# Perceiver layer with top-2 experts on one core: the first seven parts of the output copy put out one at a time

## The chip, the cores and the metric

One core of one Trainium2 chip runs the whole kernel. The metric is the device time of one execution in microseconds (us). Times of the kernel before are the median of three runs; the profile and the trace come from one further execution, taken by the hardware profiler.

## What is computed

The input x is 64 sequences of 64 tokens of 256 numbers, so 4096 tokens. Three blocks with a residual each follow one another, all in float32:

```python
x = x + xattn(layernorm(x), ctx_768, Wq, Wk, Wv, Wo, bo)  # 16 heads of 64, context 256 x 192 per sequence
x = x + attn(layernorm(x), wq, wk, wv, wo)                # causal, 16 heads of 64
x = x + ffn(layernorm(x), router, gating, up, down)       # 8 experts, the 2 likeliest per token, SiLU(gate) * up, then down
```

In the ffn block each token's result is the sum of its two experts' results, each scaled by its weight.

## The kernel before

The work goes through three stages. In the first (cross attention, to about 1090 us) and the second (self attention with the router, to about 1925 us) the tokens go through in tiles of 128. The second stage leaves two things in HBM for the third. `acc` is an array of all tokens with their residual values, to which the experts' results are added. `xs` holds the normalized token rows sorted by expert, each expert's rows in the order of the tokens, each row with its token number and its weights as tags.

The third stage is the function `moe`, in which the change lies. It runs over 67 tiles of 128 rows of `xs`, expert by expert; how many tiles an expert has is found on the chip and read from small tables in SBUF with `value_load`. The engines share it as follows.

- SP (the sync engine's queue) loads the tiles. Before it loads a tile it waits (line 1773, 1776 or 1780) until the Vector engine has copied an earlier one out of the two-tile buffer `e_xs_in`, so it keeps step with the computation until the very last tile; two loads past the last tile close the series (lines 1779 to 1781).
- PE (TensorE), ACT (ScalarE) and DVE (VectorE) compute each tile's gate, up and down products. ACT writes the weighted result to one half of `e_ys` (line 1909), after a wait until POOL has taken the token numbers of the tile before (`s_out_now`, line 1908).
- POOL (GpSimd) adds each tile's 128 result rows to `acc` with one indirect DMA that accumulates (line 1808, called "an add" from here on). It begins with a wait for the add before it to land (line 1799), so that the adds form a chain. Each add raises the semaphore `s_added` (`e_ys_added`) by 16 when it has landed.
- SP, when all its loads are out, copies `acc` to the output `out_x` in eight parts of 512 tokens, 512 KB each, from HBM to HBM (lines 1784 to 1793, "parts" from here on, numbered 0 to 7). Before each part it reads from the table `part_done` how many adds must have landed before those tokens are final, and waits for that count on `s_added`. This can be before the last add, since the last expert's rows are in the order of the tokens. Part 7 waits for all adds. A last wait holds until all eight parts have landed (`s_out`, line 1793).

`part_done` is worked out on the Vector engine at the end of the second stage (lines 1657 to 1662). SP's order is that of the program: what stands behind a wait isn't issued until the wait is over. DMAs that SP has issued are in flight together.

Of the kernel before, what the change touches and what calls it, by code (L numbers as in the profile page):

```python
# [28 lines left out]
DMA = 16  # L29
PARTS_OUT = 8  # L30
# [1638 lines left out]
def moe(nc, sem, sbuf, psum, xs_dram, s_scat, ident, raw, s_raw, load_piece, split, pads, tables, shape, acc,  # L1669
# [26 lines left out]
    with ExitStack() as ph:  # L1696
# [4 lines left out]
        with ExitStack() as ex:  # L1701
# [23 lines left out]
            s_weight, s_out_now, s_out = sem("e_weight_kept"), sem("e_token_out_set"), sem("out_stored")  # L1725
            out_gate, s_out_gate = sbuf(ex, "e_out_gate", [P, 1]), sem("e_out_gate_done")

            def tile_count(eng):
                return eng.value_load(first_tile[0:1, EXPERTS:EXPERTS + 1], min_val=MIN_TILES * EXPERTS, max_val=MAX_TILES)
# [23 lines left out]
            @block.sync  # L1753
            def _(sp):
                def load_tile(i, row, landed):
                    sp.dma_start(xs_in[:, bass.ds(i % 2 * ROW, ROW)],
                                 xs_tiles[bass.ds(row, 1)].rearrange("t p r -> p (t r)")).then_inc(landed, DMA)

                sp.wait_ge(s_scat, (4 * GROUPS + 1) * DMA)
                load_tile(0, 0, s_xs)  # L1760
                load_tile(1, 1, s_xs_second)
                sp.wait_ge(s_wlo, PIECES)
                for c in range(PIECES):
                    load_piece(sp, 1, c)
                start = 0
                for e in range(EXPERTS):
                    bound = dict(min_val=MIN_TILES * (e + 1), max_val=MAX_TILES - MIN_TILES * (EXPERTS - 1 - e))
                    end = sp.value_load(first_tile[0:1, e + 1:e + 2], **bound)
                    shift = sp.value_load(region[0:1, e:e + 1], min_val=0, max_val=(TILES + 1) * e) if e else 0
                    if e == 1:  # L1770
                        sp.wait_ge(s_scat, DMA * (4 * GROUPS + EXPERTS))
                    for i in range(0 if e else 2, MIN_TILES):
                        sp.wait_ge(s_moved, start + i)
                        load_tile(start + i, start + i + shift, s_xs)
                    with sp.Fori(start + MIN_TILES, end) as i:
                        sp.wait_ge(s_moved, i)
                        load_tile(i, i + shift, s_xs)
                    start = end
                for i in range(2):
                    sp.wait_ge(s_moved, start + i)  # L1780
                    load_tile(start + i, i, s_xs)
                for c in range(PIECES):
                    sp.wait_ge(s_raw[c], DMA * EXPERTS)
                part = NTOK // PARTS_OUT
                for c in range(PARTS_OUT):
                    if c + 1 < PARTS_OUT:
                        sp.wait_ge(s_added, sp.value_load(part_done[0:1, c:c + 1], min_val=DMA * MIN_TILES * (EXPERTS - 1),
                                                          max_val=DMA * MAX_TILES))
                    else:
                        sp.wait_ge(s_added, DMA * tile_count(sp))  # L1790
                    sp.dma_start(out[c * part:(c + 1) * part, :].rearrange("(b r) d -> b (r d)", b=32),
                                 acc[c * part:(c + 1) * part, :].rearrange("(b r) d -> b (r d)", b=32)).then_inc(s_out, DMA)
                sp.wait_ge(s_out, PARTS_OUT * DMA)
# [221 lines left out]
```

## Time and profile before

| what | us |
|---|---|
| median of three runs | 2300.44 |
| lowest and highest run | 2297.36, 2302.71 |
| the profiled execution's own time | 2298.02 |
| its span in the trace | 2296.3 |
| PE busy | 2176.0 (95%) |
| DVE busy | 1555.2 (68%) |
| ACT busy | 1301.2 (57%) |
| POOL busy | 914.2 (40%) |

The span is what lies between the first and the last event of the trace; the execution's own time is 1.7 us longer. The busy shares are means over all three stages. The change touches only the last 30 us, after the last load of a tile, and in those last 30 us PE's work comes to its end.

### The profile page before, as it was taken

The numbers are of one execution on the slowest core, as the hardware profiler recorded it, in microseconds if no ns is written. First come the engines' busy times: TensorE is split into PE (matmuls) and PEld (weight loads), VectorE is DVE, ScalarE is ACT, GpSimd is POOL, SyncE is SP. The second block draws the span as 40 slices with busy tenths as digits, with TensorE's granted clock in tenths as the row PEclk, the third lists the DMA queues.
The fourth block names the chain that finished last, engine by engine and source line by source line (L and its number), as shares of the span: only waits on it lengthen the run. The fifth ranks groups of instructions, "written<-read, shape, count | busy, mean of one in ns | idle before, by whom it ended". The sixth has DMA issues, their size and how long they took to land. (4 is left out here: it accounts for less than half of the span.)

```text
span 2296.3 us, 56727 instructions
## 1 busy us (share of the span) xinstructions
PE 2176.0 (95%) x19008; PEld 1980.3 (86%) x19008; DVE 1555.2 (68%) x3525; ACT 1301.2 (57%) x3925; POOL 914.2 (40%) x1409
## 2 busy tenths in 40 slices
PE   6999999999999999999996999999999994999996
PEld 5899999999999999999995899999999983888885
DVE  6666676767676666667654888888888874444442
ACT  5555555555555555555553777777677762545442
POOL 3333333333333333333332225555555554444443
PEclk9999999999999999999997999999999996999998
DMA  4000000000000000000005200000000003444434
GB/s 120 22 20 28 9 27 18 27 11 25 27 18 27 9 27 18 27 9 27 14 6 172 104 11 16 22 21 19 23 19 21 22 25 105 100 82 97 81 63 108
DMA packets 63901, 93.55 MB, mean 41 GB/s; under 512 B 6824, under 2 KB 47144, under 8 KB 63528
## 3 DMA queue, kind: packets, MB, share of 16 engines
q1 hardware_dynamic: 44280, 64.49, 8.8%
q0 software_dynamic: 13104, 18.56, 4.6%
q10 hardware_dynamic: 6432, 9.44, 1.4%
q8 instruction: 44, 0.72, 0.1%
q14 instruction: 41, 0.34, 0.0%
HBM read 65.39 MB, written 36.83 MB: 45 GB/s over the span
## 5 line engine op out<-in xcount | busy, mean ns | idle before, releaser
L424 POOL TENSOR_TENSOR p_sb<-p_sb,rinv 128x512 f32<-128x512 f32 x256 | 279.0, 1090 | 780.0 <-DVE rinv L770 780.0
L679 ACT ACTIVATE p_sb<-s_ps,nmax 128x256 f32<-128x256 f32 x512 | 238.1, 470 | 198.7 <-DVE nmax L745 194.9
L745 DVE TENSOR_REDUCE nmax<-s_ps 128x2 f32<-128x512 f32 x256 | 176.1, 688 | 186.1 <-PE s_ps L67 181.7
L1090 POOL TENSOR_TENSOR sp_sb<-sp_sb,srinv 128x512 f32<-128x512 f32 x128 | 133.1, 1040 | 228.8 <-DVE srinv L1444 226.7
L1340 ACT ACTIVATE sp_sb<-sm_sb,snmax 128x128 f32<-128x128 f32 x512 | 199.6, 391 | 5.6 <-DVE snmax L1459 2.6
L767 DVE COPY pt_sb<-t_ps 128x512 f32<-128x512 f32 x256 | 176.8, 690 | 22.2 <-PE t_ps L567 8.4
L48 ACT ACTIVATE q_sb<-m_ps 64x256 fp32r<-64x256 f32 x256 | 96.8, 378 | 164.4 <-PE m_ps L67 160.6
L47 ACT CAST qk_hi<-qk_ps 128x512 fp32r<-128x512 f32 x218 | 129.6, 595 | 95.6 <-PE qk_ps L67 87.7
L567 PE MATMUL t_ps<-ident,p_sb 128*128 128x128 f32 x1024 | 153.6, 273 | 2.1 <-POOL p_sb L424 1.1
L67 PE MATMUL sqk_ps<-e_w_hi 128*128 128x256 f32 x512 | 147.8, 289 | 7.2 <-DVE e_w_lo L59 7.2
L567 PEld LDWEIGHTS t_ps<-ident,p_sb 128*128 128x128 f32 x1024 | 125.1, 141 | 31.6 <-issue 4.4
L650 ACT COPY v_sb<-v_ps 128x512 f32<-128x512 f32 x256 | 149.4, 584 | 1.5 <-PE v_ps L67 1.5
L67 PE MATMUL s_ps<-cx_hi,qk_hi 128*128 128x256 f32 x512 | 148.2, 289 | 0.0
L67 PE MATMUL sqk_ps<-e_w_lo,e_w_hi 128*128 128x256 f32 x512 | 145.5, 284 | 0.0
L67 PE MATMUL sqk_ps<-e_w_hi,e_w_lo 128*128 128x256 f32 x512 | 145.4, 284 | 0.0
L67 PE MATMUL qk_ps<-q_sb,wkt_hi 128*128 128x256 f32 x436 | 131.4, 323 | 14.3 <-DVE qk_hi L59 5.9
L67 PE MATMUL s_ps<-cr_lo,qk_hi 128*128 128x256 f32 x512 | 144.9, 283 | 0.0
L67 PE MATMUL s_ps<-cx_lo,qk_hi 128*128 128x256 f32 x512 | 144.8, 283 | 0.0
L67 PE MATMUL s_ps<-cx_hi,qk_lo 128*128 128x256 f32 x512 | 144.6, 283 | 0.0
L67 PE MATMUL s_ps<-cr_hi,qk_hi 128*128 128x256 f32 x512 | 144.6, 282 | 0.0
L583 PEld LDWEIGHTS o_ps<-pt_sb,v_sb 128*64 128x64 f32 x4096 | 126.1, 139 | 11.5 <-issue 10.5
L583 PE MATMUL o_ps<-pt_sb,v_sb 128*64 128x64 f32 x4096 | 135.0, 225 | 0.8 <-DVE pt_sb L767 0.8
(340 smaller groups left out, 7465.7 us busy)
## 6 DMA issues: line engine op xcount, KB each, us to landing
e_xs_in<-xs SPq DMA_DIRECT2D x69, 132.5 KB, 2.1
ctx_raw<-in_ctx_t SPq DMA_DIRECT2D x32, 256.0 KB, 2.8
ctx_raw<-in_ctx_t SPq DMA_DIRECT2D x64, 128.0 KB, 2.9
xs<-blank_rows SPq DMA_DIRECT2D x8, 662.5 KB
x_ring<-in_x SPq DMA_DIRECT2D x16, 256.0 KB, 2.8
x_mid<-x_ring SPq DMA_DIRECT2D x16, 256.0 KB, 2.2
acc<-x_sb SPq DMA_DIRECT2D x16, 256.0 KB, 2.1
out_x<-acc SPq DMA_DIRECT2D x8, 512.0 KB, 5.3
```

The source lines that it names most:

```text
L47: return nc.scalar.copy(hi, src)
L48: return nc.scalar.mul(hi, src, scale)
L67: mm = pe.matmul(out, lhs, rhs, start=(i == 0), stop=(i == len(pairs) - 1))
L424: nc.gpsimd.tensor_tensor(prob, prob, inv, ALU.mult).then_inc(norm_done, 1)
L567: mm = pe.transpose(t_ps[:, k * P:(k + 1) * P], p_sb[:, (p - 3) % 4, k * P:(k + 1) * P], ident[:])
L583: mm = pe.matmul(o_ps[h * HEAD:(h + 1) * HEAD, c:c + HEAD], v_sb[:, k, q * P + h * HEAD:q * P + (h + 1) * HEAD], pt_sb[:, PT_SLOT[q], k * ...
L650: nc.scalar.copy(v_sb[:, p % 4, p // 4 * HALF:(p // 4 + 1) * HALF], v_ps[:]).then_inc(v_done, 1)
L679: ex = nc.scalar.activation(p_sb[:, k, b * J:(b + 1) * J], s_ps[1 - w][:, b * J:(b + 1) * J], ACT.Exp, bias=nmax[:, k, b:b + 1], scale=1.0 ...
L745: nc.vector.tensor_reduce(nmax[:, (p - 1) % 4, :], s_ps[1 - w][:].rearrange("p (b j) -> p b j", b=2), AX_X, ALU.max, negate=True).then_inc ...
L767: nc.vector.tensor_copy(pt_sb[:, PT_SLOT[(p - 3) % PAIRS], :], t_ps[:]).then_inc(t_done, 1)
L1090: nc.gpsimd.tensor_tensor(prob, prob, inv, ALU.mult).then_inc(norm_done, 1)
L1340: ex = nc.scalar.activation(p_sb[:, s, k * P:(k + 1) * P], sm_sb[:, w, k * P:(k + 1) * P], ACT.Exp, bias=nmax[:, s, k:k + 1], scale=1.0, a ...
```

## The change

For parts 1 to 6, SP waits until all parts put out before have landed, ahead of everything else it does for that part. `s_out` rises by 16 with each part that has landed, so the wait for part c is for 16 times c. Part 0 gets no such wait, and part 7 none either: it still has its wait for all the adds alone.

```diff
                 part = NTOK // PARTS_OUT
                 for c in range(PARTS_OUT):
+                    if c and c + 1 < PARTS_OUT:
+                        sp.wait_ge(s_out, DMA * c)
                     if c + 1 < PARTS_OUT:
                         sp.wait_ge(s_added, sp.value_load(part_done[0:1, c:c + 1], min_val=DMA * MIN_TILES * (EXPERTS - 1),
                                                           max_val=DMA * MAX_TILES))
```

Two places show it in SP's own list of instructions. The first is the start of the output copy. `out_stored` is the semaphore `s_out`, `e_ys_added` is `s_added`, and the TENSOR_LOAD with the two ISA rows behind it is the `value_load` of one entry of `part_done`. Before:

```order
 L1756 DMA e_xs_in<-xs 128x265
 L1787 TENSOR_LOAD part_done [waits e_raw_loaded2,e_raw_loaded1,e_raw_loaded0]
 L1787 ISA x2
 L1791 DMA out_x<-acc 16x8192 [waits e_ys_added]
 L1787 TENSOR_LOAD part_done
 L1787 ISA x2
 L1791 DMA out_x<-acc 16x8192 [waits e_ys_added]
```

Now:

```order
 L1756 DMA e_xs_in<-xs 128x265
 L1789 TENSOR_LOAD part_done [waits e_raw_loaded2,e_raw_loaded1,e_raw_loaded0]
 L1789 ISA x2
 L1793 DMA out_x<-acc 16x8192 [waits e_ys_added]
 L1789 TENSOR_LOAD part_done [waits out_stored]
 L1789 ISA x2
 L1793 DMA out_x<-acc 16x8192 [waits e_ys_added]
```

No instruction is added: the new wait sits on the TENSOR_LOAD of the second part's count, so that this load too comes after the landing. The rows of the four parts that follow read like the last three.

The second place is the end of SP's list, from the seventh part (part 6) on. Before:

```order
 L1787 TENSOR_LOAD part_done
 L1787 ISA x2
 L1791 DMA out_x<-acc 16x8192 [waits e_ys_added]
 L1729 TENSOR_LOAD first_tile
 L1729 ISA x2
 L1790 REGISTER_ALU
 L1791 DMA out_x<-acc 16x8192 [waits e_ys_added]
 L1701 UNCONDITIONAL_BRANCH [waits out_stored]
```

Now:

```order
 L1789 TENSOR_LOAD part_done [waits out_stored]
 L1789 ISA x2
 L1793 DMA out_x<-acc 16x8192 [waits e_ys_added]
 L1729 TENSOR_LOAD first_tile
 L1729 ISA x2
 L1792 REGISTER_ALU
 L1793 DMA out_x<-acc 16x8192 [waits e_ys_added]
 L1701 UNCONDITIONAL_BRANCH [waits out_stored]
```

Part 6 has the new wait, part 7 is as it was, behind part 6 in the queue. The lists of the other engines are unchanged but for line numbers.

## Rows read from the trace of the kernel before

**Rows 1.** The page: its span, and the last section, DMA issues (median landing).

```profile
span 2296.3 us, 56727 instructions
...
acc<-x_sb SPq DMA_DIRECT2D x16, 256.0 KB, 2.1
out_x<-acc SPq DMA_DIRECT2D x8, 512.0 KB, 5.3
```

**Rows 2.** Waits of SP's queue, from 2267 us to the end.

```profile
SPq L1791 <- DMA acc<-e_ys,e_token_out: 14.3, 2, 8.9
SPq L1701 <- DMA out_x<-acc: 4.6, 1, 4.6
SPq L1756 <- DVE e_xs L1947: 4.5, 1, 4.5
```

**Rows 3.** Chain that ended last, from 2235 us: start us, us, what.

```profile
2264.17 3.87 DMA acc<-e_ys,e_token_out
...
2269.17 10.39 DMA acc<-e_ys,e_token_out
...
2280.69 4.00 DMA acc<-e_ys,e_token_out
```

**Rows 4.** Timelines of POOL, ACT and PE near the end: start us, us, instruction.

```profile
2285.83 1.58 POOL L1808 DMA_INDIRECT acc<-e_ys,e_token_out  x1 [0.33 <-issue]
```

```profile
2280.42 0.47 ACT L1909 ACTIVATE e_ys<-e_y_ps,slot_tags 128x256 f32 x1 [6.35 <-POOL e_token_out L1803]
```

```profile
2276.22 0.28 PE L67 MATMUL e_y_ps<-e_w_lo,e_ht_hi 128*128 128x256 f32 x1
```

**Rows 5.** Timeline of SP: output copies, merged where they follow closely.

```profile
2268.40 0.64 SPq L1791 DMA_DIRECT2D out_x<-acc  x1
...
2269.66 1.69 SPq L1791 DMA_DIRECT2D out_x<-acc  x2
...
2279.58 0.51 SPq L1791 DMA_DIRECT2D out_x<-acc  x1
...
2289.55 1.72 SPq L1791 DMA_DIRECT2D out_x<-acc  x2
```

**Rows 6.** Line 1791, one window per part: parts 0, 1, 5, 6, 7.

```profile
L1791 SPq DMA_DIRECT2D out_x<-acc x1: 643/643/643, 2268.4 to 2268.4; - x1
DMA to landing us min/median/max: 4.1/4.1/4.1
...
L1791 SPq DMA_DIRECT2D out_x<-acc x1: 546/546/546, 2269.7 to 2269.7; - x1
DMA to landing us min/median/max: 5.5/5.5/5.5
...
L1791 SPq DMA_DIRECT2D out_x<-acc x1: 514/514/514, 2279.6 to 2279.6; - x1
DMA to landing us min/median/max: 4.0/4.0/4.0
...
L1791 SPq DMA_DIRECT2D out_x<-acc x1: 521/521/521, 2289.5 to 2289.5; - x1
DMA to landing us min/median/max: 3.9/3.9/3.9
...
L1791 SPq DMA_DIRECT2D out_x<-acc x1: 515/515/515, 2290.8 to 2290.8; - x1
DMA to landing us min/median/max: 5.1/5.1/5.1
```

**Rows 7.** Line 1787, the value loads: ns min/median/max, first and last start.

```profile
L1787 SPq TENSOR_LOAD <-part_done x7: 266/269/280, 2267.8 to 2280.1; - x7
L1787 SPq FUSED_REGOPS  x7: 147/147/176, 2268.1 to 2280.4; - x7
```

**Rows 8.** Windows around part 5; last columns: granted clock, DMA share, GB/s.

```profile
2279.50:2280.50 1.00, 0.00 (x0) 0.00 (x0) 0.00 (x0) 0.08 (x1) 0.50 (x3) 1.00 0.00 0
2280.50:2282.00 1.50, 0.00 (x0) 0.00 (x0) 0.00 (x0) 0.39 (x1) 1.31 (x1) 0.68 0.98 350
2282.00:2282.50 0.50, 0.00 (x0) 0.00 (x0) 0.00 (x0) 0.00 (x0) 0.25 (x1) 0.50 0.00 0
2282.50:2284.50 2.00, 0.00 (x0) 0.00 (x0) 0.00 (x0) 0.00 (x0) 0.00 (x0) 0.50 0.59 66
```

## The prediction

> **What bounds the end now.** The page gives the span, 2296.3 us [rows 1]. PE is the busiest engine over the whole of it, but the change touches only SP's last instructions, so I read the end of the trace. First SP's waits [rows 2]: from 2267 us on, SP waits 4.5 us for the last tile load's buffer, then twice for adds to `acc`, 14.3 us together, then 4.6 us for the output copy to land. What ends last is therefore the output copy, and before it the adds. The chain [rows 3] shows the adds, one behind the other. Most land 3.8 to 4.0 us after they are issued, and the next is issued some 1.1 us later. One stands out: the add issued at 2269.17 landed after 10.39 us, at 2279.56.
>
> SP's timeline [rows 5] says what lay beside it. Part 0 went out at 2268.40, when SP had finished its loads; part 1 at 2269.66, part 2 1.17 us behind it (1.69 less its own 0.52), and parts 3 and 4 at like distances, so by about 2273.2. These five were in flight together with the slow add. Part 5 went out at 2279.58, when that add had landed, and part 6 at 2289.55. Between them two more adds ran, issued at 2280.69 [rows 3] and 2285.83 [rows 4]; part 6 left when the last had landed, 3.7 us after its issue. Part 7 followed at 2290.75 (2289.55 plus 1.72 less 0.52), landed 5.1 us later at 2295.85 [rows 6], and the span ended 0.45 us after that. PE was done at 2276.5 [rows 4]. So the end of the program is: the burst of five parts slows one add by 6.5 us, the adds end at 2289.55, and the last two parts follow.
>
> **The change, part by part.** The new wait leaves part 0 at 2268.40: it has none, and SP's loads ahead of it are untouched. What goes away is the burst. The add at 2269.17 then has only part 0 beside it, and I price it at 3.9 us like the others of [rows 3]. It lands at 2273.1, the next is issued 1.1 us later at 2274.2 and lands at 2278.1, the last is issued at 2279.2 and lands at 2283.1. Its data is there: PE ended at 2276.5, and ACT's last copy to `e_ys`, now at 2280.42 after 6.35 us of waiting for POOL [rows 4], would come by 2277. The adds thus end 6.5 us sooner. That is the gain, if SP could use it.
>
> What is added is a chain on SP. Each of parts 1 to 6 starts only when the part before has landed. Nothing else is queued behind SP's wait but the remaining parts, and no engine waits for SP there, so only the end is touched. One step of the new chain has two terms.
>
> The first is a part's landing. [Rows 6] has it for three parts that had no other part ahead of them: 4.1 us (part 0), 4.0 (part 5), 3.9 (part 6). Part 1, with part 0 and an add beside it, took 5.5 us. Can one part beside one add keep 4.0? Around part 5 the windows [rows 8] show no DMA work for about 1 us after its issue at 2279.58, then 1.5 us at a share of 0.98, then nothing for 0.5 us, then the work of the add issued at 2280.69, at a share of 0.59. A part moves its data 1 to 2.5 us after issue, an add from about 1.8 to 3.8 us after. In the new schedule parts leave every 4.65 us and adds every 5.0 us, and the phases fall beside one another: part 1 leaves at 2273.1, add 66 (the one before the last) at 2274.2, which is the distance of part 5 and its add. I take 4.1 for part 0 and 4.0 for parts 1 to 5. The nearest rows bound it from both sides: 3.9 and 5.5.
>
> The second term is what SP does between that landing and the next issue. Before, this lay beside the flight of the part ahead and cost the end nothing; now its cover is gone, since the wait sits on the load of the count. It takes 0.62 us: part 0's issue ended at 2269.04 (2268.40 plus 0.64), part 1's began at 2269.66 [rows 5]. The TENSOR_LOAD is 0.27 of it and the register work 0.15 [rows 7]. With 0.03 for waking from the wait (part 5 left at 2279.58, the add had landed at 2279.56) I take 0.65. The Trainium skill's page DMA: Bandwidth & Descriptors, section Latency and other measured facts, gives a floor of about 600 ns for a tensor_load; this trace disagrees, with 0.27 us, and by the page the sum would be about 2.0 us higher.
>
> Sum: part 6 leaves at 2268.40 + 4.1 + 5 x 4.0 + 6 x 0.65 = 2296.4. By then all adds have long landed, so the waits on them cost nothing. Part 7 leaves 1.2 us later, at 2297.6, as before: its wait is for adds alone. It lands after 5.1 us, again with part 6 just ahead, at 2302.7, and the end comes 0.45 us later, at 2303.15. Against 2296.3 that is **6.85 us more**. The adds' 6.5 us fall out of the path: their end moves from 2289.55 to 2283.1, and part 6 wouldn't have left before 2296.4 anyway.
>
> The profiled execution took 2298.02 us in all, so its like would be 2304.9. It lies 2.4 us below the median of the runs, 2300.44; I add the change to the median: **2307.3 us**.
>
> **The rivals.**
>
> *The parts hold each other up less than the landings say: no difference.* The break-even is easily had: part 6 must leave at 2289.55, so a step must take (2289.55 - 2268.40) / 6 = 3.52 us and a landing 2.88. For it speaks that a copy of 256 KB from SBUF to `acc` lands in 2.1 us [rows 1]; with the data phase of 1.5 us for 512 KB [rows 8], half of it for 256 KB, that leaves 1.35 us of fixed time, and 1.35 + 1.5 = 2.85 us for a part. The sum would be 6 x 2.85 + 3.9 = 21.0 us, part 6 at 2289.4, the end 0.15 us earlier than now: 2300.3. Against it: this very copy has three rows of its own, none under 3.9 us, and part 5 had the DMA engines to itself while it moved.
> The Trainium skill's page DMA: Bandwidth & Descriptors, section Anatomy of one DMA, fits 2.0 us plus the bytes at 436 GB/s, measured on POOL's path; for 512 KB that is 3.2 us, and by it the sum would be 1.9 us more than now, within what can be told from no change. The trace's 3.9 to 4.1 us disagree. I give the whole case 0.06.
>
> *Faster: the adds set the end.* If a part lands as fast as that 256 KB copy, in 2.1 us, a step is 2.75 us and part 6 leaves at 2284.9, behind the adds' new end at 2283.1. The end comes 4.65 us sooner: 2295.8. The mechanism is the slow add of 10.39 us, which becomes 3.9; it decides from landings under 2.88 us down, and at 1.8 us the adds bound the end. For it: the burst did cost that add 6.5 us, and the adds were on the path. Against it: the same three rows. 0.03.
>
> *Slower still: parts and adds collide.* If the two series drift into one another, three of the parts that are in flight while adds run (parts 0 to 3) take part 1's 5.5 us in place of 4.0, 4.5 us more: 2311.8. For it: part 1's row, and the burst's effect on the add. Against it: that took several parts at once, and the phases above leave room. 0.07.
>
> *The wait does nothing.* It would if the count were already there when SP comes by. It isn't: only parts raise it, part 0 lands 4.1 us after its issue, and SP is back after 0.64. I give it no chance of its own.
>
> **How the numbers follow.** The forecast gets 0.84. Its own bounds are small: all landings at 3.9 take 0.7 us off, two parts at 5.5 add 3.0. The three runs of before lie up to 3.1 us from their median, so a median may be 2 to 3 us off. The range reaches from 2303.5 (the forecast less 0.7 and less 3.1) to 2311.8, the collision's time, which also covers two slowed parts with a little of the spread. It leaves out the two cases without a loss, 0.09 together, and the far end of the collision.
>
> A measurement of this kernel tells about 0.2%, 4.6 us, from no change. The forecast's 6.85 us is 0.30%, so some of its chance, 0.04, falls within 0.2% through the spread of the runs. Slower: 0.84 - 0.04 + 0.07 = 0.87. Same: 0.06 + 0.04 = 0.10. Faster: 0.03.
>
> **What the new profile would show.** Eight output copies on SP's timeline, the first at the same distance from the last tile load, seven of them some 4.65 us apart and the eighth 1.2 us behind the seventh. SP waiting for the output copy on the line of the value load six times, 3.4 us each (a landing less the issue's own 0.52), and once more at the end for 4.6; no wait left for adds. Landings of 4.0 us for the first six parts. No add above some 4.5 us, the last landed near 2283 us. The span near 2303. I'd be wrong in the size if landings are 5 us or more while adds run, and wrong in the sign if they are under 2.9 us, with SP then waiting for adds ahead of part 6 again.

## The result and the profile after

| | before | with the change |
|---|---|---|
| median of 8 runs, us | 2300.72 | 2306.41 |
| lowest and highest run | 2296.03, 2304.95 | 2304.26, 2309.52 |
| ratio, 95% interval | | 1.0030 [1.0021, 1.0039] |
| the profiled execution's own time | 2298.02 | 2308.73 |
| its span | 2296.3 | 2307.0 |

The change makes the kernel slower: by 5.7 us (0.25%) by the medians, by 0.30% by the ratio, and the whole interval lies above 0.2%. The forecast was 6.85 us more. One single execution of the kernel before, among those beside the experiments, took 6515.68 us; the ratios leave it out. The two spans differ by 10.7 us, which is too much: the last stage already began 3.0 us later in the profiled execution of after. SP's timeline of before has its first tile load at

```profile
1925.92 0.85 SPq L1756 DMA_DIRECT2D e_xs_in<-xs  x2
```

and that of after at

```profile
1928.91 0.85 SPq L1756 DMA_DIRECT2D e_xs_in<-xs  x2
```

with 2.0 us more by the end of the tiles. None of that work has changed, and the single runs of before are spread over 9 us as well. So all traces are compared from here on by **T, the time from the issue of part 0 to the end of the span**. For before, T = 2296.3 - 2268.40 = 27.9 us [rows 5]. For after, SP's timeline (start us, us) has

```profile
2273.35 29.05 SPq L1793 DMA_DIRECT2D out_x<-acc  x8
...
2300.69 1.72 SPq L1793 DMA_DIRECT2D out_x<-acc  x2
```

and T = 2307.0 - 2273.35 = 33.65 us, 5.75 us more, which is what the medians say. The second row is parts 6 and 7: part 6 left 27.34 us after part 0, where before it took 21.15. That is six steps of 4.56 us on average. The waits of SP's queue from 2267 us on (us in total, times, longest), which answer to [rows 2]:

```profile
SPq L1789 <- DMA out_x<-acc: 20.5, 6, 3.5
SPq L1756 <- DVE e_xs L1949: 8.7, 2, 4.5
SPq L1701 <- DMA out_x<-acc: 4.2, 1, 4.2
SPq L1793 <- DMA acc<-e_ys,e_token_out: 1.1, 2, 0.5
```

Before, SP waited 14.3 us for adds; now it waits 20.5 us for its own copies, on the line of the value load, and by this view hardly for adds. Two of the eight parts in the view of line 1793, part 1 and part 7, which answer to [rows 6]:

```profile
L1793 SPq DMA_DIRECT2D out_x<-acc x1: 546/546/546, 2278.0 to 2278.0; - x1
DMA to landing us min/median/max: 3.9/3.9/3.9
...
L1793 SPq DMA_DIRECT2D out_x<-acc x1: 515/515/515, 2301.9 to 2301.9; - x1
DMA to landing us min/median/max: 4.7/4.7/4.7
```

Part 1 lands in 3.9 us in place of 5.5; all of parts 0 to 6 are between 3.9 and 4.1. The adds, in the chain of waits, which answers to [rows 3]:

```profile
2269.16 3.86 DMA acc<-e_ys,e_token_out
2274.15 4.32 DMA acc<-e_ys,e_token_out
2279.59 3.79 DMA acc<-e_ys,e_token_out
```

The add of 10.39 us is gone. The one that has part 0 beside it takes 4.32 us, the next 3.79. The last was issued at 2284.52, 11.2 us after part 0, and before at 17.4 us. The last add landed 6.2 us sooner, counted from part 0, and it bought nothing.

### The profile page after: what moved, and what is told of

Read it like the earlier page. It is cut to its first block and busy times, and to the rows that moved or that the text cites. A ratio compares the mean times of both kernels' runs of the same rounds, so it can differ in the third digit from the quotient of the medians.

```text
span 2307.0 us, 56727 instructions
## 1 busy us (share of the span) xinstructions
PE 2177.6 (94%) x19008; PEld 1981.7 (86%) x19008; DVE 1556.4 (67%) x3525; ACT 1306.4 (57%) x3925; POOL 915.1 (40%) x1409
```

## The experiments

The theory under test is that of the prediction. Beside the adds, copies in flight together slow an add; after the adds, copies that wait for one another lose the overlap of their fixed times. The change pays for the first with the second. The main rivals were that the slow add has another cause, that the step is set by something else than landing plus count, and that the DMA engines' rate bounds the end whatever the order. All edits are to the loop over the parts. In the table, "against before" is the difference of the medians, since before was run beside each group on the same chip. T is read from one execution of each kernel. Its differences agree with those of the medians within 1.3 us, but mostly show the larger gain, so the medians are the safer measure of what a schedule is worth.

| run | T, us | against before, us | ratio, 95% interval |
|---|---|---|---|
| before | 27.9 | | |
| the change | 33.65 | +5.7 | 1.0030 [1.0021, 1.0039] |
| the change again | 33.7 | +5.0 | 1.0024 [1.0013, 1.0034] |
| count read first | 31.1 | +3.9 | 1.0017 [1.0008, 1.0026] |
| all adds first | 29.85 | +2.0 | 1.0007 [0.9998, 1.0017] |
| two in flight | 26.0 | -2.1 | 0.9993 [0.9984, 1.0002] |
| two in flight, count first | 26.1 | -1.0 | 0.9994 [0.9985, 1.0003] |
| the change's wait, parts 1 to 3 | 25.3 | -1.4 | 0.9994 [0.9985, 1.0003] |
| parts 1 to 3, count first | 24.5 | -2.7 | 0.9985 [0.9976, 0.9994] |
| parts 1 and 2, count first | 24.4 | -2.7 | 0.9988 [0.9979, 0.9997] |
| four parts of 1 MB, no waits | 26.9 | +0.3 | 1.0005 [0.9996, 1.0014] |
| four parts of 1 MB, waits | 24.7 | -2.1 | 0.9993 [0.9984, 1.0001] |
| halves of 256 KB, waiting (one execution) | 47.95 | +21.4 | |
| early parts | | -5.8 | 0.9972 [0.9962, 0.9983] |

**1. The count read ahead of the wait.**

```diff
-                    if c and c + 1 < PARTS_OUT:
-                        sp.wait_ge(s_out, DMA * c)
                     if c + 1 < PARTS_OUT:
-                        sp.wait_ge(s_added, sp.value_load(part_done[0:1, c:c + 1], min_val=DMA * MIN_TILES * (EXPERTS - 1),
-                                                          max_val=DMA * MAX_TILES))
+                        count = sp.value_load(part_done[0:1, c:c + 1], min_val=DMA * MIN_TILES * (EXPERTS - 1),
+                                              max_val=DMA * MAX_TILES)
+                        if c:
+                            sp.wait_ge(s_out, DMA * c)
+                        sp.wait_ge(s_added, count)
```

> T is the time from the issue of part 0 to the end of the span: 27.9 us before, 33.65 us with the change. Here each part still waits for the one ahead of it to land, but SP reads the part's count before that wait, beside the flight. Theory (the added time is a chain of six steps, a landing of 3.9 us plus SP's 0.62 us each): a step falls from 4.56 to about 3.95 us, T to about 30.0 us, the time about 2.2 us above before and 3.6 us under the change. Rival 1 (the landing alone sets the step, the count costs nothing): T stays at 33.6. Rival 2 (parts that come sooner meet the adds' data and land later): steps of 4.4 us or more while adds run, T of 31 to 33 us, adds of 4.5 us and more.

SP's timeline, the eight parts and the last two of them, in a span of 2300.9 us:

```profile
2269.80 26.60 SPq L1794 DMA_DIRECT2D out_x<-acc  x8
...
2294.69 1.71 SPq L1794 DMA_DIRECT2D out_x<-acc  x2
```

Part 6 left 24.89 us after part 0, a mean step of 4.15 us, where 3.95 was expected, and T is 31.1, not 30.0. But the steps aren't alike. Parts 2 to 5 left at

```profile
2277.84 0.51 SPq L1794 DMA_DIRECT2D out_x<-acc  x1
...
2282.34 0.51 SPq L1794 DMA_DIRECT2D out_x<-acc  x1
...
2286.86 0.52 SPq L1794 DMA_DIRECT2D out_x<-acc  x1
...
2290.73 0.51 SPq L1794 DMA_DIRECT2D out_x<-acc  x1
```

Four of the six steps, those behind parts 0, 1, 4 and 5, take 3.9 to 4.1 us, as the theory has it: a landing and next to nothing behind it. So the count's whole path, 0.6 us a step, is saved, and rival 1 falls. The two steps behind parts 2 and 3 take 4.5 us. Both parts left 1.1 to 1.5 us behind an add. The add beside part 3 was slowed as well:

```profile
L1811 POOL DMA_INDIRECT acc<-e_ys,e_token_out x1: 1580/1580/1580, 2281.3 to 2281.3; - x1
DMA to landing us min/median/max: 5.7/5.7/5.7
```

That is rival 2: two steps above 4.4 us, one add of 5.7 us and the first of 4.71, T within its 31 to 33 us. It holds for two parts of six and makes up the 1.1 us that T lies above the theory.

**2. Parts 1 to 7 wait for all the adds.** In the kernel before, only the first line of the condition changes, to `if c < 1:`, so that every part but part 0 waits for the full count.

> T is the time from the issue of part 0 to the end of the span: 27.9 us before, 33.65 us with the change. Here parts 1 to 7 wait for all the adds and then go out in a burst without waits for landings; part 0 is as before. Theory (the slow add of 10.39 us comes from the burst alone): every add lands in 3.7 to 4.4 us and the last one 15 us after part 0; the burst of seven then takes about 12.4 us (4.0 for the first, 1.4 for each further), T about 27.9 us, the time the same as before within 1 us. Rival (the slow add comes from its place in the program and not from the burst): an add of over 7 us remains and T is 33 us or more.

Waits of SP's queue, span 2298.8 us, part 0 at 2268.95:

```profile
SPq L1791 <- DMA acc<-e_ys,e_token_out: 13.9, 1, 13.9
SPq L1701 <- DMA out_x<-acc: 6.6, 1, 6.6
```

The chain has the adds behind part 0:

```profile
2269.57 4.75 DMA acc<-e_ys,e_token_out
2275.44 3.82 DMA acc<-e_ys,e_token_out
```

No add above 4.75 us: the slow add came from the burst, and the rival falls. Part 1 left at 2284.2, 15.2 us after part 0, as foreseen. What was off is the burst of seven: it landed 14.2 us after that and not 12.4. So T is 29.85 us and the median 2.0 us above before, where the same within 1 us was expected. The landings grew from 4.1 to 7.1 us, so a part came in every 1.7 us. The DMA engines were full meanwhile, and PE and the others idle (the last three columns are clock, DMA share, GB/s):

```profile
2285.50:2294.00 8.50, 0.00 (x0) 0.00 (x0) 0.00 (x0) 0.00 (x0) 0.00 (x0) 0.50 0.99 335
```

**3. Two parts in flight.** Two semaphores in turn, and part c waits for part c - 2:

```diff
+                    if c >= 2 and c + 1 < PARTS_OUT:
+                        sp.wait_ge(s_out[c % 2], DMA * (c // 2))
```

> T is the time from the issue of part 0 to the end of the span: 27.9 us before, 33.65 us with the change. Here a part waits for the landing of the part two ahead of it (two semaphores in turn), so at most two are in flight. Theory (the serial landings bound the change, the burst's slow add bounds before): two parts in flight land in 5.1 to 5.5 us, a pair of parts takes about 6 us, part 6 leaves 17 to 18 us after part 0, the adds end 15 to 16 us after it, each within 4.6 us. T about 24.5 us, the time about 3 us under before. Rival (two parts in flight already slow the adds as five did): one add of 7 us or more, the adds end 18 us or later, T of 27 us or more, no gain over before.

Chain of waits and SP's last two parts, span 2292.3 us, part 0 at 2266.26:

```profile
2266.85 6.31 DMA acc<-e_ys,e_token_out
2274.29 6.79 DMA acc<-e_ys,e_token_out
```

```profile
2285.92 1.72 SPq L1793 DMA_DIRECT2D out_x<-acc  x2
```

Between theory and rival: two adds took 6.3 and 6.8 us, so two parts in flight do slow an add, by 2.5 to 3 us each. Part 6 waited for the last add and left after 19.7 us, where I had said 17 to 18. T is 26.0, where I had said 24.5. It is under before in the trace; in the runs the interval takes in no change.

**4. The same with the count read first.**

> T is the time from the issue of part 0 to the end of the span: 27.9 us before, 33.65 us with the change. Here at most two parts are in flight, as in the run with two in flight, and SP reads the count before the wait. Theory: a pair of parts takes about 5.4 us, part 6 leaves about 16.5 us after part 0, T about 23.3 us, the time 4 to 5 us under before. Rival (the adds now end last, or two parts always in flight slow them): part 6 waits for adds, the adds take 5 us or more each, T of 25 us or more, no better than with the count behind the wait.

```profile
2270.67 6.16 DMA acc<-e_ys,e_token_out
2277.96 7.01 DMA acc<-e_ys,e_token_out
```

SP waited 7.4 us for the last add ahead of part 6, and T is 26.1, not 23.3. The rival holds: the adds are the later of the two here, and parts that leave sooner buy nothing. The slow adds take 6.2 and 7.0 us, where they took 6.3 and 6.8 in run 3.

**5. Only parts 1 to 3 wait, count first.** As in 1, with `if 1 <= c <= 3:`.

> T is the time from the issue of part 0 to the end of the span: 27.9 us before, 33.65 us with the change, 31.1 us with the change and the count read first. Here only parts 1 to 3 wait for the landing of the part ahead (with the count read before the wait), the others go as before the change. Theory (one part at a time leaves the adds nearly alone, and what costs time is only the serial chain once the adds are over): part 3 leaves 12.4 us after part 0, parts 4 and 5 just behind it, only the last add meets them and takes up to 8 us, part 6 leaves at 17 to 19 us, T of 23.5 to 25.5 us, the time 2.5 to 4 us under before. Rival (any three parts together cost the adds what the burst of five did): the last add takes 10 us or more and T is 27 us or more, no better than before.

Waits of SP's queue, span 2292.4 us, part 0 at 2267.94:

```profile
SPq L1794 <- DMA out_x<-acc: 9.0, 3, 3.4
SPq L1701 <- DMA out_x<-acc: 6.2, 1, 6.2
```

T is 24.5, and the ratio's interval lies below 1. SP waits for no add at all any more. The last add takes 3.7 us and lands 15.0 us after part 0; part 6 leaves at 16.2, sooner than the 17 to 19 expected, since that add met the parts without being slowed. The rival falls.

**6. The change's own wait, for parts 1 to 3 alone.** The change with `if 1 <= c <= 3:` as its condition.

> T is the time from the issue of part 0 to the end of the span: 27.9 us before, 33.65 us with the change, 24.5 us where parts 1 to 3 alone wait and read their count first. Here the change's own wait stands as the change has it, ahead of the count, but only for parts 1 to 3; parts 4 to 6 have none. Theory (the change's loss is in the last three waits, its gain for the adds in the first three): part 3 leaves 13.7 us after part 0 (3 x 4.56), the adds take 3.7 to 4.5 us, T is 25 to 26 us, the time 2 to 3 us under before. Rival (the gain of the other run came from reading the count first): T of 27.5 us or more, no gain over before.

```profile
2272.12 19.27 SPq L1793 DMA_DIRECT2D out_x<-acc  x8
```

With a span of 2297.4, T is 25.3, within the 25 to 26 expected, and the rival's 27.5 is out. Here the change's waits are split in two. Its first three waits take 2.6 us off T (27.9 to 25.3), its last three add 8.35 us (25.3 to 33.65). The runs show the first only as 0.9994 [0.9985, 1.0003], so as a gain of the program it isn't shown by this run alone. The last three are: the change again (run 12), beside it on the same chip, has a median 6.45 us above this run's.

**7. Only parts 1 and 2 wait, count first.**

> T as in the other runs. Here only parts 1 and 2 wait for the part ahead, count read first. Theory (DMAs that are in flight together share the engines, so a burst beside an add costs it some 1.6 us for each 512 KB part ahead of it): parts 3 to 5 leave 9.3 to 11.7 us after part 0 and meet the last add, which takes 7 to 9 us; part 6 leaves at 19 to 20.5 us, T of 25 to 27 us, 1 us or so worse than with three waits. Rival (the DMA engines' rate alone bounds the end, whoever goes first): T within 0.5 us of 24.5 us or under it.

POOL's last add, and SP's last two parts, span 2296.3 us, part 0 at 2271.93:

```profile
2282.73 1.58 POOL L1811 DMA_INDIRECT acc<-e_ys,e_token_out  x1 [0.33 <-issue]
```

```profile
2290.01 1.71 SPq L1794 DMA_DIRECT2D out_x<-acc  x2
```

The last add met parts 3 to 5 and landed just before 2290.01, so after 7.3 us, within the 7 to 9 expected. But part 6 left 18.1 us after part 0 and not after 19 to 20.5, and T is 24.4, as with three waits and not 25 to 27. So here the theory's time missed and the rival's came out. Its mechanism isn't shown by that. At the 1.7 us a part of run 2, eight parts would be 13.6 us (an estimate), and SP still waited 5.5 us for the last add ahead of part 6. With two waits part 6 leaves 1.8 us later than with three (18.1 against 16.2 us), but parts 3 to 5 have landed by then, and what follows takes 6.3 us in place of 8.3. T comes to 24.4 to 24.7 us by three schedules (runs 5, 7 and 9).

**8. Halves of 256 KB, each waiting.** Each part is put out as two DMAs, with 13 waits for landings.

> T as in the other runs. Here each part is put out as two halves of 256 KB, and each half before part 7 waits until all before it have landed: 13 waits in place of 6. Theory (a landing is a fixed time of 2.4 us and a data phase of 1.5 us for 512 KB): a half lands in 3.1 to 3.3 us and T is about 51 us, 17 us more than with the change. Rival 1 (a landing goes by the bytes): halves land in 2.0 us and T is 35 us, as with the change. Rival 2 (2.0 us fixed and the bytes at 436 GB/s): halves in 2.6 us, T about 43 us.

Of line 1796, a half without an add beside it, and one with an add:

```profile
L1796 SPq DMA_DIRECT2D out_x<-acc x1: 509/509/509, 2299.8 to 2299.8; - x1
DMA to landing us min/median/max: 2.9/2.9/2.9
```

```profile
L1796 SPq DMA_DIRECT2D out_x<-acc x1: 517/517/517, 2276.8 to 2276.8; - x1
DMA to landing us min/median/max: 3.7/3.7/3.7
```

The span was 2318.0, part 0 left at 2270.05, T is 47.95, where about 51 was expected. Halves land in 2.8 to 3.1 us alone, below the 3.1 to 3.3 of the theory and above the 2.6 of rival 2. Rival 1 is out. With 2.9 us for 256 KB and 3.9 for 512 KB, the doubling costs 1.0 us, and what doesn't scale is about 1.9 us (an estimate from the two). One execution, so no interval; but 14 us more than the change is far beyond the spread.

**9. Four parts of 1 MB, waiting, and 10. not waiting.** `PARTS_OUT = 4` in the change and in the kernel before.

> T as in the other runs. Here the output copy has four parts of 1 MB, of which parts 1 and 2 wait for the landing of the part ahead and part 3 for the adds alone. Theory (2.4 us fixed, 3.0 us of data for 1 MB, and only two waits): parts land in 5.4 us alone and up to 6.5 beside adds, part 2 leaves at 12 to 14 us, the adds end at 17 us, T of 22.5 to 25.5 us, 2.5 to 5 us under before in the time. Rival (a 1 MB part holds up the adds as the burst did): adds of 7 us and more, part 3 leaves after 20 us, T of 27 us or more.

> T as in the other runs. Here the output copy has four parts of 1 MB and none waits for a landing, as in the kernel before. Theory (what is in flight together slows the add, whatever the size of the parts): parts 0 to 2 go out within 2.5 us, one add takes 10 to 12 us, part 3 leaves at 21 to 23 us, T of 27 to 29.5 us, the time within 1.5 us of before; then the wait for landings is a gain with four parts where it was a loss with eight. Rival (fewer and larger parts are better by themselves): T under 26 us here too.

Waiting (span 2294.6, part 0 at 2269.89), the adds behind part 0 in the chain:

```profile
2270.60 5.79 DMA acc<-e_ys,e_token_out
2277.51 5.18 DMA acc<-e_ys,e_token_out
```

Not waiting (span 2298.9, part 0 at 2272.01):

```profile
2272.62 8.96 DMA acc<-e_ys,e_token_out
2282.70 5.12 DMA acc<-e_ys,e_token_out
```

Part 2 of the second run left only at 2281.6, when its count was there, so its burst was two parts of 1 MB and not three, and its slow add took 8.96 us in place of 10 to 12. T is 26.9 without waits and 24.7 with them: with four parts the wait takes 2.2 us off, with eight it adds 5.75. The wait still helps the adds: the last lands 2.1 us sooner after part 0 (18.6 against 20.7 us), where with eight parts it was 6.2. The rest is that there are two waits in place of six, and part 3 leaves with the last add in both, so none of the waits stands behind the adds. Both rivals fall: no add above 5.8 us with the waits, and no T under 26 us without them. A 1 MB part landed in 5.2 to 5.7 us in the run that waits. The medians say the same, -2.1 and +0.3, but the two intervals overlap.

**11. The parts ahead of the last loads.** SP waited 4.5 us for the last tile load [rows 2], and nearly as long for the one before it (8.7 us for both in the view of the change). Here part 0 goes out ahead of the wait for the last load but one and part 1 ahead of the wait for the last; parts 1 to 4 wait for the part ahead, count first.

```diff
                 for i in range(2):
+                    put_out(i)
                     sp.wait_ge(s_moved, start + i)
                     load_tile(start + i, i, s_xs)
...
+                for c in range(2, PARTS_OUT):
+                    put_out(c)
```

> Here part 0 goes out ahead of SP's wait for the last load but one, part 1 ahead of the wait for the last load (into the 4.5 us that SP waits there), and parts 1 to 4 wait for the part ahead, count read first. Measured from the issue of the last tile load to the end of the span: 29.0 us before (2267.3 to 2296.3), 34.7 with the change, 25.5 us with three waits. Theory: part 2 takes the place of part 0, parts 3 and 4 follow at 4.15 us each, part 5 behind them meets no add's data, part 6 leaves with the last add 15.5 us after part 2, the end comes 22.5 to 24 us after the last load, the time 4 to 5 us under before. Rival (a part beside a tile load holds up the load, and with it PE): the loads take 4 us or more, PE's last matmul comes later than 9.2 us after the last load, and the gain is under 2 us.

SP's timeline, span 2292.9 us:

```profile
2261.21 0.64 SPq L1790 DMA_DIRECT2D out_x<-acc  x1
2264.93 0.35 SPq L1756 DMA_DIRECT2D e_xs_in<-xs  x1
2265.96 0.55 SPq L1790 DMA_DIRECT2D out_x<-acc  x1
2269.99 0.35 SPq L1756 DMA_DIRECT2D e_xs_in<-xs  x1
...
2286.57 1.71 SPq L1790 DMA_DIRECT2D out_x<-acc  x2
```

The end came 22.9 us after the last load, part 6 left 15.46 us after part 2 (issued at 2271.11), both as the theory had it; the last add, with parts 4 and 5 in flight, took 4.3 us. The median is 5.8 us under before, 0.9972 [0.9962, 0.9983], more than the 4 to 5 expected and the best of the runs. Not all of it comes from the early parts: from the last load to the end before took 29.0 us, three waits with the count first 25.5, and this run 22.9. So the early parts are worth 2.6 us on top of the spacing. Alone, without the waits, they weren't run. The loads keep their distance of 5.06 us. PE's last matmul did end 10.4 us after the last load, where it was 9.2 before, which was the rival's sign. But its last product started as before, 7.5 us after the load; it took longer because the granted clock had fallen. Windows of this run (length, PE busy and the other engines; the last three columns are clock, DMA share, GB/s):

```profile
2275.00:2277.40 2.40, 0.47 (x5) 0.23 (x3) 0.66 (x1) 1.06 (x2) 0.50 (x3) 1.00 0.95 263
2277.40:2280.50 3.10, 2.93 (x12) 2.63 (x12) 0.03 (x1) 0.00 (x0) 1.56 (x1) 0.51 0.33 37
```

0.51 is about 1.2 GHz; in the window ahead, with PE idle for most of 2.4 us, it was still at its full 2.4 GHz. The early parts aren't needed for that. Run 1, which has none, shows the same, with PE's end 10.15 us after the last load:

```profile
2276.20:2278.90 2.70, 2.65 (x12) 2.35 (x12) 0.00 (x0) 0.00 (x0) 1.56 (x1) 0.57 0.25 24
```

The kernel before has the same pause of 2.0 us ahead of the last product and stays at 1.00, so why the clock falls in some executions is open. It cost nothing here, since the last add was issued at 2282.28, 1.9 us after PE's end and right behind the add ahead of it.

**12. The change again**, beside runs 6, 7 and 11.

> The change again, on the chip of the three other runs. T 33 to 34 us, landings of 3.9 to 4.1 us for the parts that have no other part beside them, steps of 4.5 to 4.6 us, the time 5 to 7 us above before. If the time were within 2 us of before, the 5.7 us of the first comparison would be chance in the stages ahead.

T is 33.7 us (2303.3 - 2269.58), the median 5.0 us above before, landings 3.9 to 4.1 but for part 7's 4.8. The loss isn't chance.

## Why the prediction was right

- **What bounds the end: right.** The burst slows one add, the adds hold part 6, two parts follow. Run 2 shows the burst's part in it, run 6 what is to be had without it.
- **The adds' gain falls out of the path: right.** The last add was issued 6.3 us sooner, counted from part 0 (17.43 to 11.17). I had priced the add beside part 0 at 3.9 us like its neighbours; it took 4.32, and 4.33 to 4.75 in the other runs where part 0 alone was beside it. This was off the path.
- **The step: right in kind, a little large.** I had 4.65 us (4.75 for the first); it was 4.56. Landings of 4.0 were 3.9 to 4.1. The 0.65 us between landing and next issue was 0.6: part 0 landed 4.03 us after its issue and part 1 left after 4.62. All of it hangs on the count. With the count read first, in run 7, part 0 landed after 4.2 us and part 1 left after 4.19. Part 6 left after 27.34 us, I had said 28.0.
- **Part 7: mis-sized.** I kept its landing of 5.1 us; it was 4.7, and 4.6 to 4.8 in the four other traces that tell it and where no burst lay ahead. The 0.4 us together with the 0.66 of the steps is the whole difference between T as forecast, 34.75 us, and as measured, 33.65.
- **The waits for adds: nearly.** I had none left. The view names two of 0.5 us, ahead of parts 1 and 2. But part 1 left at 2278.0 and the add then in flight landed at 2278.47 (2274.15 plus 4.32), and with part 2 it is likewise, so no add's landing let them go. What the two stand for is open; the steps there aren't longer than the others by that much.
- **The rivals.** No collision: parts 1 to 3 landed in 3.9 to 4.1 us while adds ran. That hung on the phases, as the prediction said, and not by much: in run 1 parts 1 to 3 leave 0.8 to 1.5 us sooner against the adds, and parts 2 and 3 take 4.5 us. No shorter landings in an emptier machine either: the shortest landing of 512 KB in any run is 3.85 us (part 5 of run 12). So my 2.85 us from the copy out of SBUF doesn't hold for a copy from HBM to HBM. Nor does the fit of the Trainium skill, DMA: Bandwidth & Descriptors, section Anatomy of one DMA (2.0 us plus the bytes at 436 GB/s for POOL's path, so an estimate of 3.2 us for this part). For 256 KB and 1 MB the estimates from it are 2.6 and 4.4 us, and the runs show 2.8 to 3.1 and 5.2 to 5.8.

What I didn't see is that the wait is a gain and a loss that can be parted. The sum treated it as one thing with one sign. The first three waits are a gain in T of 2.6 us, the last three a loss of 8.35 (1.4 and 6.45 by the medians).

## What to carry to other kernels

A wait that spaces DMAs out protects what shares the engines with them, but only while that runs: put it where the other stream is still on the path, and end it there. Each transfer that waits for the one ahead pays the whole landing time (3.9 us here, of which only about half grows with the bytes) and whatever the queue does between wait and issue, so do that ahead of the wait. A new distance between transfers also moves them against the other stream: the sum of a step holds only for the phase that it was read from. Look too for time in which the issuing queue waits anyway: two parts moved into SP's waits for tile loads took 2.6 us off on top of the spacing.

## What the runs showed of the hardware

The price of copies beside an indirect add, from all traces (before's add behind part 5 with them):

| beside the add | the add lands after, us |
|---|---|
| no part | 3.7 to 3.9 |
| one 512 KB part, left 0.6 to 0.8 us ahead of the add | 4.3 to 4.75 |
| one 512 KB part, left 1.1 us behind the add | 5.7 (run 1 alone) |
| one half of 256 KB, left 1.0 us behind the add | 4.9 (run 8 alone) |
| one 512 KB part at a time, none of them less than 1.1 us ahead or 1.5 us behind | 3.6 to 4.0 |
| two or three parts at once | 6.2 to 7.3 |
| the same, both left 1.9 us or more ahead (run 11), or 1.5 us or more behind (run 5) | 4.3, 3.7 |
| a burst of five | 10.4 |
| one 1 MB part | 4.7 to 5.8 |
| two 1 MB parts | 9.0 |

So the distance between the two issues matters as much as the copy being in flight. The part pays as well: in runs 1 and 5 the steps behind parts that had left 1.1 to 1.8 us behind an add were 4.5 us, where the others were 3.9 to 4.1. A copy of 512 KB from HBM to HBM landed in 3.85 to 4.1 us with nothing beside it, and in a burst of seven a part came in every 1.7 us.
